# Graph network on one core: the stages between the edge passes rewritten

## What is computed

```python
edge_index = jnp.stack([src, dst])
x = _layernorm(x + _L0_gnn_ref(x, edge_index, edge_weight), axis=-1)      # weighted sum over dst
x = _layernorm(x + _L1_gnn_ref(x, edge_index, edge_attr_5, ...), axis=-1)  # softmax over src, 2 heads
x = _layernorm(x + _L2_gnn_ref(x, edge_index, edge_attr_32, ...), axis=-1) # attention softmax over dst, 2 heads, MLP
x = _layernorm(x + _L3_gnn_ref(x, edge_attr_3, ...), axis=-1)              # spline weights, mean over dst, batch norm
```

## Time and profile before

| | us |
|---|---|
| median of three runs | 11246.22 (11240.04 to 11255.09) |
| the profiled execution | 11246.92 |
| its span | 11245.1 |
| DVE busy | 7124.9 (63%) |
| POOL busy | 6918.7 (62%) |
| ACT busy | 4592.4 (41%) |
| PE busy | 3078.5 (27%) |

### The profile page before, as it was taken

The page is one execution under the profiler, slowest core; times in us unless marked ns, Lnnn a source line. Parts: engine busy times, 40 slices in busy tenths (PEclk is TensorE's granted clock), DMA queues, the critical chain, the costliest instruction groups (busy, mean ns, idle before and its releaser), DMA issues. The chain is left out here.

```text
span 11245.1 us, 92785 instructions
## 1 busy us (share of the span) xinstructions
PE 3078.5 (27%) x20703; PEld 2546.4 (23%) x20703; DVE 7124.9 (63%) x9873; ACT 4592.4 (41%) x5918; POOL 6918.7 (62%) x6628
## 2 busy tenths in 40 slices
PE   1111366573000000000004566666664720000000
PEld 1111366563000000000003355555553310000000
DVE  6767788886311222118995488888885357777775
ACT  0111255452011111116772377777773234444441
POOL 6777787664577777770002577777773057777774
PEclk9999977776555555555555577777775555555555
DMA  3232322221333332224551344444441067777773
GB/s 98 78 75 89 86 64 68 70 70 51 50 111 107 111 111 103 102 100 184 200 206 43 92 136 130 128 135 129 129 135 52 23 200 235 235 235 235 235 234 90
DMA packets 722526, 1395.98 MB, mean 124 GB/s; under 512 B 409267, under 2 KB 439162, under 8 KB 714834
## 3 DMA queue, kind: packets, MB, share of 16 engines
q0 software_dynamic: 287136, 587.26, 19.4%
q1 hardware_dynamic: 406318, 636.04, 17.1%
q10 hardware_dynamic: 28996, 171.86, 4.1%
HBM read 827.48 MB, written 602.51 MB: 127 GB/s over the span
## 5 line engine op out<-in xcount | busy, mean ns | idle before, releaser
L740 POOL DMA_INDIRECT l_rows<-in_x,l_idx x1568 | 1954.3, 1246 | 669.1 <-issue 490.7
L2180 POOL DMA_INDIRECT l_rows<-table,l_idx x1568 | 1499.5, 956 | 926.9 <-issue 472.6
L1719 POOL DMA_INDIRECT l_rows<-h,l_idx x1568 | 1564.6, 998 | 614.3 <-issue 475.9
L1123 POOL DMA_INDIRECT rows<-l_rows,l_idx x1568 | 1522.6, 971 | 537.0 <-issue 497.0
L1748 PE MATMUL l_made<-l_kv_w,l_rows_t 97*128 97x256 f32 x3136 | 1139.6, 522 | 781.5 <-ACT l_kv L1778 472.4
L2255 ACT ACTIVATE l_lifted<-l_rows,l_up 128x256 f32<-128x256 f32 x1568 | 639.6, 460 | 1041.6 <-DMA l_rows<-table,l_idx 1041.6
L1748 PEld LDWEIGHTS l_made<-l_kv_w,l_rows_t 97*128 97x128 f32 x3136 | 784.2, 267 | 996.4 <-issue 852.5
L1511 PE MATMUL l_wide<-l_diag,l_ones 128*128 128x384 f32 x4 | 3.3, 928 | 3144.9 <-DVEq L1538 3144.9
L1113 DVE TENSOR_TENSOR l_rows<-l_run,l_weights_ps 128x56 f32<-128x56 f32 x56 | 12.0, 215 | 1340.9 <-POOLq L88 1340.7
L1080 ACT COPY l_rows<-l_run 128x1792 f32<-128x1792 f32 x56 | 190.7, 3405 | 1578.5 <-POOLq L88 1569.6
L826 ACT COPY l_out<-l_run 128x1792 f32<-128x1792 f32 x56 | 190.4, 3401 | 1339.5 <-DVE l_run L776 1339.5
(11 more groups left out here) (366 smaller groups left out, 12787.7 us busy)
## 6 DMA issues: line engine op xcount, KB each, us to landing
sums<-l1s_out ACTq DMA_DIRECT2D x56, 1988.0 KB, 6.6
sums<-l_out SPq DMA_DIRECT2D x112, 924.0 KB, 4.5
spread<-zeros SPq DMA_DIRECT2D x28, 3612.0 KB, 12.9
l_spread<-spread SPq DMA_DIRECT2D x112, 903.0 KB
l1s_rows<-rows SPq DMA_DIRECT2D x56, 1008.0 KB, 5.7
spread<-zeros SPq DMA_DIRECT2D x56, 938.0 KB
l_spread<-spread SPq DMA_DIRECT2D x56, 938.0 KB, 4.6
sums<-l_out ACTq DMA_DIRECT2D x56, 896.0 KB, 3.7
```

The costliest lines, as they stand in the source:

```text
L740: pool.indirect_dma_start(rows[:, b, t], None, a["x"], bass.IndirectOffsetOnAxis(ap=idx[:, b, t:t + 1], axis=0)) \
L1123: pool.indirect_dma_start(g["rows1_d"], bass.IndirectOffsetOnAxis(ap=idx[:, b, t:t + 1], axis=0), rows[:, b, t], None).then_inc(sent[b], 16)
L1719: pool.indirect_dma_start(rows[:, c.r, t, 0:C], None, g["h2_d"], bass.IndirectOffsetOnAxis(ap=idx[:, c.r, t:t + 1], axis=0)).then_inc(got[ ...
L2180: pool.indirect_dma_start(rows[:, b, t], None, g["table3_d"], bass.IndirectOffsetOnAxis(ap=idx[:, b, t:t + 1], axis=0)) \
```

## The change

- Gathers are issued and waited for in two parts of 24 and 25 tiles (`HALF_TILES`), in both collects, and DVE works on the first part while POOL issues the second. `collect_sums` has four PSUM banks and adds layer 0's residual itself. `collect_softmax` has six banks of three tiles; DVE multiplies them into a buffer `joined` of 12 tiles and adds that at once, and the reciprocals and products of the next block (`means`) are made per part at its end.
- `Normalise` takes the place of `normalise`: every operation in two parts, and ScalarE squares. The copies ahead of it in layer 2 are gone.
- Layer 1's weights are multiplied out in the first block of the program. The node tables are made in two parts; POOL's order is 49 rows of the first table, 24 of the second, the two head rows, one DMA that adds the bias row to the output weights, then 25 rows. ACT copies the features into the second table.
- The three clears of layer 1's edge pass move into the node tables' block, the six of the source order pass to the end of the edge pass's DVE program. Layer 1's output weights and bias are loaded in the node tables' block.
- Layer 1's finish works on pairs of tiles, through `Pipeline`. The output weights and the copied tiles have 128 partitions in place of 70, with zeros. The other uses of `Pipeline` keep one tile at a time. In layer 2 the eight loads stay at the start of their block, with no work of DVE's left ahead of the wait for them.

The diff, cut to its core. `Normalise`:

```diff
+HALF_TILES = (slice(0, 24), slice(24, NT))
...
-        v.tensor_tensor(sums, sums, stat[:, 0].unsqueeze(2).to_broadcast([P, NT, C]), ALU.subtract)
+        for at in HALF_TILES:
+            v.tensor_tensor(centred[:, at], sums[:, at], wide(stat[:, 0], at), ALU.subtract).then_inc(self.centred, 1)
+        for n, at in enumerate(HALF_TILES):
+            v.wait_ge(self.squared, 2 * turn - 1 + n)
+            v.tensor_reduce(stat[:, 1, at], work[:, at], AX, ALU.add)
...
-        v.tensor_tensor(work, sums, sums, ALU.mult)
...
-        v.tensor_reduce(stat[:, 1], work, AX, ALU.add)
...
-        v.tensor_scalar(stat[:, 1], stat[:, 1], 1.0 / C, LN_EPS, ALU.mult, ALU.add).then_inc(centred, 1)
...
+        act.wait_ge(self.summed, turn)
+        nc.scalar.activation(stat[:, 2], stat[:, 1], ACT.Sqrt).then_inc(self.rooted, 1)
```

`collect_sums`:

```diff
+                for n, at in enumerate(HALF_TILES):
+                    for i in range(at.start, at.stop):
+                        pool.indirect_dma_start(total[:, i], None, sums_d,
+                                                bass.IndirectOffsetOnAxis(ap=g["end_idx"]["dst"][:, i:i + 1], axis=0)).then_inc(got[n], 16)
...
                 for n, group in enumerate(groups):
-                    if n >= 2:
-                        pe.wait_ge(read, n - 1)
+                    if n >= 4:
...
-                v.wait_ge(got, 16 * NT)
-                v.tensor_tensor(total[:], total[:], g["filled"]["dst"][:].unsqueeze(2).to_broadcast([P, NT, C]), ALU.mult)
-                v.drain()
...
+                for n, at in enumerate(HALF_TILES):
+                    v.wait_ge(got[n], 16 * (at.stop - at.start))
+                    v.tensor_tensor(total[:, at], total[:, at],
+                                    g["filled"]["dst"][:, at].unsqueeze(2).to_broadcast([P, at.stop - at.start, C]), ALU.mult)
+                    v.drain()
+                    for m, group in enumerate(groups):
+                        if at.start <= group[0] < at.stop:
+                            v.wait_ge(mult, m + 1)
+                            of = slice(group[0], group[-1] + 1)
+                            v.tensor_tensor(total[:, of], total[:, of], more[:, m % 4, 0:len(group)], ALU.add).then_inc(read, 1)
+                    if residual is not None:
+                        v.drain()
+                        v.tensor_tensor(total[:, at], total[:, at], residual[:, at], ALU.add)
     return total
```

Node tables, POOL's order and the clears of layer 1:

```diff
+                    v.memset(out_w[:], 0.0).then_inc(zeroed, 1)
+                    v.memset(rows_a[:, :, H:], 1.0)
...
-                            v.tensor_tensor(prod[:], x[:], node_w[:, side, h, 0:C].unsqueeze(1).to_broadcast([P, NT, C]), ALU.mult)
+                        for at in HALF_TILES:
+                            for h in range(H):
+                                v.tensor_tensor(prod[:, h, at], x[:, at], node_w[:, side, h, 0:C].unsqueeze(1).to_broadcast([P, at.stop - at.start, C]),
+                                                ALU.mult)
                             v.drain()
-                            v.tensor_reduce(score[:, side, h], prod[:], AX, ALU.add)
+                            for h in range(H):
+                                v.tensor_reduce(score[:, side, h, at], prod[:, h, at], AX, ALU.add)
                             v.drain()
-                        for h in range(H):
-                            if side == 0:
-                                v.tensor_scalar(rows_a[:, :, h], score[:, 0, h], node_w[:, 0, h, C:C + 1], None, ALU.add)
-                            else:
-                                v.tensor_scalar(rows[:, :, C + h], score[:, 1, h], const[:, h:h + 1], None, ALU.add)
-                        v.drain().then_inc(tabled, 1)
+                            for h in range(H):
+                                if side == 0:
+                                    v.tensor_scalar(rows_a[:, at, h], score[:, 0, h, at], node_w[:, 0, h, C:C + 1], None, ALU.add)
+                                else:
+                                    v.tensor_scalar(rows[:, at, C + h], score[:, 1, h, at], const[:, h:h + 1], None, ALU.add)
+                            if side == 1:
+                                v.memset(rows[:, at, B1 - 1:], 1.0)
+                            v.drain().then_inc(tabled, 1)
...
+                    v.memset(keep[:], 0.0)
+                    v.memset(edge_rows[:], 1.0)
+                    v.memset(run[:], 0.0)
...
-                        pool.wait_ge(tabled, n + 1)
-                        for i in range(NT):
...
-                    pool.wait_ge(saved, 32)
...
+                        for m, at in enumerate(HALF_TILES):
+                            pool.wait_ge(tabled, n * 2 + m + 1)
+                            if n == 1 and m == 0:
+                                pool.wait_ge(copied, 1)
+                            if n == 1 and m == 1:
+                                pool.wait_ge(saved, 32)
+                                pool.indirect_dma_start(head[:], None, g["table1_d"],
+                                                        bass.IndirectOffsetOnAxis(ap=g["head_key"]["dst"][:], axis=0)).then_inc(fetched, 16)
+                                pool.indirect_dma_start(head_a[:], None, g["tablea_d"],
+                                                        bass.IndirectOffsetOnAxis(ap=g["head_key"]["src"][:], axis=0)).then_inc(fetched, 16)
+                                pool.wait_ge(weights_in, 16)
+                                pool.dma_start(out_w[F1 - 1:F1], a["out1_bias"], accum_op=ALU.add).then_inc(biased, 16)
+                            for i in range(at.start, at.stop):
+                                pool.indirect_dma_start(g[target], bass.IndirectOffsetOnAxis(ap=g["start_idx"][k][:, i:i + 1], axis=0),
+                                                        table[:, i], None, bounds_check=EP - 1, oob_is_err=False).then_inc(fetched, 16)
...
-                    v.memset(keep[:], 0.0)
-                    v.memset(rows[:], 1.0)
-                    v.memset(run[:], 0.0)
...
+                    held.clear(v)
...
+    def clear(self, v):
+        for t in (self.hold, self.hold_keep, self.scale, self.run):
+            v.memset(t[:], 0.0)
+        v.memset(self.fresh[:], -FAR)
+        v.memset(self.top[:], -FAR)
```

`collect_softmax`:

```diff
+    W, BANKS = H * F, 6
+    groups = [range(i, min(i + 3, NT)) for i in range(0, NT, 3)]
+    assert HALF_TILES[1].start % 12 == 0
+    batches = [[n for n in range(len(groups)) if i <= groups[n][0] < i + 12] for i in range(0, NT, 12)]
...
-                    nc.tensor.matmul(more[:, i % 2, 0:W], masks[:, i * P:(i + 1) * P], scaled[:], start=True, stop=True).then_inc(mult, 1)
+                for n, group in enumerate(groups):
+                    if n >= BANKS:
+                        pe.wait_ge(read, n - BANKS + 1)
...
-                for i in range(NT):
-                    v.wait_ge(mult, i + 1)
+                for n, at in enumerate(HALF_TILES):
+                    count = at.stop - at.start
+                    v.wait_ge(got[n], 16 * count)
...
-                        last = v.scalar_tensor_tensor(out=total[:, i, h * F:(h + 1) * F], in0=more[:, i % 2, h * F:(h + 1) * F],
-                                                      scalar=exps[:, 1, i, h:h + 1], in1=total[:, i, h * F:(h + 1) * F],
-                                                      op0=ALU.mult, op1=ALU.add)
-                    last.then_inc(read, 1)
...
+                        part = total[:, at, h * F:(h + 1) * F]
+                        v.tensor_tensor(part, part, exps[:, 0, at, h].unsqueeze(2).to_broadcast([P, count, F]), ALU.mult)
+                    for batch in batches:
...
+                        for m in batch:
+                            v.wait_ge(mult, m + 1)
+                            of, to = slice(groups[m][0], groups[m][-1] + 1), slice(groups[m][0] - first, groups[m][-1] + 1 - first)
+                            size = len(groups[m])
+                            v.tensor_tensor(joined[:, to].rearrange("p t (h f) -> p t h f", h=H),
+                                            more[:, m % BANKS, 0:size * W].rearrange("p (t h f) -> p t h f", t=size, h=H),
+                                            exps[:, 1, of].unsqueeze(3).to_broadcast([P, size, H, F]), ALU.mult).then_inc(read, 1)
+                        v.drain()
+                        of = slice(first, groups[batch[-1]][-1] + 1)
+                        v.tensor_tensor(total[:, of, 0:W], total[:, of, 0:W], joined[:, 0:of.stop - first], ALU.add)
+                        v.drain()
```

Layer 1's `means` and finish:

```diff
+            v.drain()
+            for h in range(H):
+                part = summed[:, at, h * F1:(h + 1) * F1]
+                v.tensor_tensor(part, part, recip[:, at, h].unsqueeze(2).to_broadcast(wide), ALU.mult)
...
+                    v.memset(turned_s[64:P], 0.0).then_inc(zeroed, 1)
                     v.tensor_tensor(acc[:], x[:], bias[:].unsqueeze(1).to_broadcast([P, NT, C]), ALU.add)
...
```

(23 more changed lines are left out.)

423 lines of the change are left out of this document (204 added, 219 removed).

## The result

| | before | changed |
|---|---|---|
| median of 4 runs | 11246.7 us (11240.0 to 11255.1) | 11100.1 us (11089.2 to 11104.4) |
| ratio, 95% interval | | 0.9868 (0.9855 to 0.9880) |
| span of the profiled execution | 11245.1 | 11098.2 |

The forecast was 11144 us with a range of 11115 to 11178. The forecast column gives the prediction's terms, added up for the same stretches. The table cuts both spans at the same instructions, and its rows follow on each other without a gap; "pass" rows hold no edited loop.

The account below looks back on a forecast made before the run. No single engine bounds the kernel; within stages the engines work one after the other. Savings and losses, with +33 in layer 1's finish, sum to -102.2 us from 11246.9: 11144 us on the median's scale, range 11115 to 11178.

Parts of the forecast that it names:

- POOL's blocking in layer 1's collect: Layer 1's softmax collect: DVE's operations with two SBUF inputs hold POOL's later gathers 7.4 us, bounds 3.7 and 10.9.
- The second rival: POOL is held for the whole of every DVE operation with two SBUF inputs: +14 us, so 11158; chance 17%.
- The clears: Clears of layer 1's edge pass (-12.2) and the source order pass (-18.2) are covered when moved: together -30 us.
- rival 4: Covers fail: clears slow POOL's spreads by 30 us, or ScalarE's squares gain nothing (20); 11164 to 11190 us; chance 12%.
- The normalisations: Six normalisations, in two parts with ScalarE squaring: -3.4 us each, -20.4 together; bounds -2.5 and -5 each.
- the loads' row: Layer 2's last block: its eight loads, issued at 8670.01 and used at 8678.18, lose their cover: +8.3 us, lower bound about 6.
- the edge passes' loops are not edited, so I take their times as unchanged: First step, on the long edge passes between the edited stages: no change in their time, 0 us.
- The prediction's own sign of being wrong: The forecast is wrong if any edge pass changes by more than 5 us, among other signs.
- Rival 3: Edge passes pay: POOL's issues 0.065 us longer cancel the gain (102), 0.09 gives 11285 us; slower; chance 3%.
- The two loads that POOL made there: Layer 1's finish: two loads by POOL, hidden by the products before and hidden after the change; no gain priced.
- the pair: Layer 1's finish: 3.7 us per pair of tiles, PE's products waiting for the copy; stage 92.4 us, a loss of +33.
- The rows of the softmax collects: Softmax collects in two parts: layer 1's -25.5 us, layer 2's -24 us, the latter before +8.3 for uncovered loads.

Follow-up runs that it names:

- sp_loads_timed: Kernel before, with the output weights and bias of layer 1's finish loaded by SyncE and not POOL, timed on another chip: 11212.9 us, ratio 0.9972.

## Why the prediction was right and wrong

**Right: the edited stages.** Eleven of the twelve edited stretches are within 4 us of the forecast, the twelfth (layer 1's finish) 4.5 off. POOL's blocking in layer 1's collect was sized well: six gathers of 1.63, 1.51, 2.46, 2.62, 2.48 and 1.51 us, 6.5 over their 0.944, where 7.4 was taken. The second rival's full price of 10.9 was not paid, although DVE's operations with two SBUF inputs ran for 11.3 us beside the gathers. The Trainium skill (page "SBUF — State Buffer", section "SBUF: two separate sides") lets a DVE operation shut GpSimd out if it has two SBUF inputs; by that rule the products L1640, which take one input from PSUM, should block nothing, and the trace agrees (issues of 0.94 and 0.95 beside them). The clears were covered on the quicker chip, rival 4 fell. The normalisations gave 2.7 to 3.2 each where 3.4 was forecast, but the one in layer 2's first block nothing: the term left out the wait for the stored table behind it. Two small slips changed nothing: the loads' row (8670.01 to 8678.18) is 8.2 us and not 8.3, and rival 4's terms add up to 11194 at most, not 11190.

**Wrong: "the edge passes' loops are not edited, so I take their times as unchanged".** This step failed, and it is most of the miss: -32.6 of the 44.7 us; without it the time would have been 11133, inside the range. The prediction's own sign of being wrong, an edge pass that changes by more than 5 us, came true twice (-19.3 and -13.3). Rival 3 did look at the place but for one sign alone, a loss. One edit did it that the prediction priced at nothing: "The two loads that POOL made there were hidden by the products before and are hidden now". Their time was hidden; moving them from POOL's program to SyncE's was worth 31 us (`sp_loads_timed`), by 1568 issues in each of two passes, 7 to 11 ns each. Why is open.

**Mis-sized: the pair.** 3.7 us was forecast and 3.50 measured: I added the hand-overs on top of PE's 1.07 and 1.90, while the next transposes start 0.2 us before the products' modelled end. That is 5 us of the finish. The rows of the softmax collects were 2 and 4 us better, that of the node tables 3, each by a little in many steps.

The range was too narrow for the reason that the first step held no term: a bound of 0.01 us on the 3136 issues of the two passes in which the issue sets the time would have added 31 us and taken the measurement in.

## What to carry to other kernels

A loop that runs 1568 times has to have a bound even if no edit touches it: read the median of its costliest instruction before and after any change, to the nanosecond; the mean can hide it (layer 2's rose from 998 to 1001 ns while the median fell from 955 to 945). Time a change on more than one chip: here the gain was 1.3% on one and 0.4% on another. In a chain of transpose, copy and product, issue the next transpose ahead of the product; with one tile or pair in hand PE pays for every copy. Work that covers a load must be looked up again when it is moved: the wait for layer 2's loads came to 8 us when their cover went into the block before.
